# First layer's edge loop: the product of keys and queries is kept in PSUM, and the next gathers wait for the product

## The chip, the cores and the metric

The kernel runs on one core of a Trainium2 chip. Its time is the device time in microseconds (us) of the whole program. TensorE (PE) multiplies matrices from SBUF into PSUM, VectorE (DVE) and ScalarE (ACT) work element by element on SBUF and PSUM, GpSimd (POOL) here mostly issues indirect DMAs (gathers by a list of row numbers), and SyncE (SP) issues plain DMAs. Each engine runs its own instructions in their written order and waits on semaphores that other engines raise.

## The reference, cut to what matters

The model has four pairs of a graph layer and an expert layer on 6250 nodes with 256 features. The first graph layer is an attention over 100,000 edges with 4 heads of 64 features. For an edge from node s to node d and a head h it takes a score q[d,h]·k[s,h] / 8, makes a softmax of the scores over all the edges that end in d, and sums the values v[s,h] with these weights into node d. So each edge needs the 256 keys and the 256 values of its source node, and the 256 queries of its target node. Everything else of the model (seven more layers) is as before and is not touched by the change.

## The kernel before, in words

The edges are sorted by target block beforehand. A tile is 128 edges, one per partition; a *quad* is `Q = 4` tiles. `edge_attend` handles `n = 208` quads. For quad q the engines do this:

- **POOL, `gather` (L2817 to L2827).** Four indirect DMAs, one for each tile, bring 512 floats per edge: first the 256 values, then the 256 keys. They land in `ring`, which has two lanes (even and odd quads, `LANE_SETS = 2`) of seven slots, 260 floats apart. A row is 512 floats long, so the keys of quad q lie where the values of quad q+2 are to go. Hence `gather` of quad q first waits until the keys of quad q-2 are no longer needed: L2819 waits for `val_ready` to count the scores of quad q-2. L2821 waits until the slot's old values have been summed.
- **DVE, `onehot` (L2988)** makes the one-hot matrices `s4` of edges against the nodes of their block.
- **PE, `turn_s` (L2891)** turns them, **ACT, `copy_st` (L2836)** copies them to SBUF, and **PE, `query` (L2900)** multiplies them with the queries: `qe` holds for every edge the queries of its target. `qe` is in PSUM and has two halves, for even and odd quads; a half is 128 x 1024 floats. L2898 waits before it overwrites the half of quad q-2.
- **DVE, `score`.** L2993 waits for the gathered rows, L2998 multiplies the keys with `qe` and puts the product over the keys in `ring` (semaphore `prod_own`), and L3001 sums 64 products for each head and edge into `val` (semaphore `val_ready`).
- Every fourth quad (`closes`), **DVE** finds the running maximum along the sorted list by scans (`within`, `across`, `under`), with small matmuls of **PE** and two exponentials of **ACT** in between. The result is a weight for each edge and head, and a factor `fade` for what has been summed so far.
- **ACT, `widen` (L2867) and `weigh` (L2876, 16 instructions, and L2877)** multiply the values in `ring` by the weights.
- **PE, `collect` (L2948)** sums the weighted values by target: for each tile of the quad one matmul into `o`, which has two banks (`BK = 2`). It waits for the addition of the tile two before (L2947).
- **DVE, `add` (L3081)** adds each of these four results to the accumulator `l_acc`; L3070 and L3072 apply `fade` on every fourth quad.

**What sets the order.** There is no planner. Each engine's program is written out by `steps` (L72): step s issues, for each stage with its lag, the work of quad s - lag. Stages that are plain functions are issued where the list is made, ahead of those that are generators; generators take turns, one piece each up to their next `yield`. So step s is, on PE: `turn_s`(s-1), the small matmuls, two `collect` matmuls of quad s-11, two `query` matmuls of quad s-2, one `collect`, two `query`, one `collect`. On DVE step s is: `onehot`(s), the product of quad s-4, the first addition (or `fade`) of quad s-12, a piece of a scan, then the reduce of quad s-4 (L3001), and the other additions and scan pieces in turn. On POOL it is `gather`(s). `lead = n + 16` means that all 208 quads are written out, with no loop on the chip. A barrier stands at the end of the phase, so the next stage begins when the last engine is done.

Of the kernel before, what the change touches and what calls it, by code (L numbers as in the profile page):

```python
# [11 lines left out]
ALU = mybir.AluOpType  # L12
ACT = mybir.ActivationFunctionType
AX = mybir.AxisListType
# [57 lines left out]
def steps(eng, n, stages, lead=4, tail=0, unroll=2, in_order=False):  # L72

    total = n + max(lag for lag, _ in stages)
    if not in_order:  # L80
        stages = sorted(stages, key=lambda s: -s[0])

    def emit(s, slot, peeled):
        turns = [fn(s - lag, (slot - lag) % unroll) for lag, fn in stages if not peeled or 0 <= s - lag < n]
        turns = [t for t in turns if t is not None]
        while turns:
            turns = [t for t in turns if next(t, turns) is not turns]

    rounds = max(0, (n - lead - tail) // unroll)
    for s in range(min(lead, total)):  # L90
        emit(s, s % unroll, True)
    if rounds:
        with eng.Fori(0, rounds) as i:
            for k in range(unroll):
                emit(i * unroll + (lead + k), (lead + k) % unroll, False)
    for s in range(lead + unroll * rounds, total):
        emit(s, s % unroll, True)
# [2003 lines left out]
def blocks_of(nc, engine, L, q, tiles=Q):  # L2101

    _, vals = nc.values_load_multi_w_load_instructions(L.block[0:1, ds(q * tiles, tiles)], engines=(engine,),
                                                       min_val=0, max_val=T - 1,
                                                       skip_runtime_bounds_check_because="made below T on chip")
    return vals
# [649 lines left out]
LANE_SETS = 2  # L2756
# [3 lines left out]
def edge_attend(nc, core, L, name, table, queries, acc, scale):  # L2760

    H, W, n, CQ, U, BK = 4, D, L.quads, 4, 14, 2
# [5 lines left out]
    with Phase(nc, name) as ph:  # L2768
        ring = ph.sb("ring", [P, LANE_SETS * Q, LANE])

        def rows(q, a, b):
            at, lane = q // LANE_SETS % LANE_SLOTS * LANE_STEP, q % LANE_SETS * Q
            return ring[:, lane:lane + Q, at + a:at + b]
# [21 lines left out]
        qe = ph.ps("qe", [P, 2, Q, W])  # L2795
# [18 lines left out]
        with nc.Block() as block:  # L2814
            @block.gpsimd
            def _(pool):
                def gather(q, slot):  # L2817
                    if q >= LANE_SETS:
                        pool.wait_ge(val_ready, q - LANE_SETS + 1)  # L2819
                    if q >= AWAY:  # L2820
                        pool.wait_ge(out_done, (q - AWAY + 1) * Q)  # L2821
                    pool.sem_inc(taken, 1)
                    for j in range(Q):
                        t = q * Q + j
                        pool.indirect_dma_start(rows(q, 0, 2 * D)[:, j, :], None, table,  # L2825
                                                bass.IndirectOffsetOnAxis(ap=L.src[:, t:t + 1], axis=0)
                                                ).then_inc(got[q % LANE_SETS], 16)  # L2827
                steps(pool, n, [(0, gather)], **whole)
# [51 lines left out]
            @block.tensor  # L2880
            def _(pe):
                for k in range(2):
                    pe.matmul(o[0:1, k, 0:half], core.ident[:, P - 1:P], L.dst[:, k * half:(k + 1) * half],
                              start=True, stop=True).then_inc(lasts, 1)

                def turn_s(q, slot):
                    pe.wait_ge(s_ready, q + 1)
                    if q:
                        pe.wait_ge(st_ready, q)
                    for j in range(Q):  # L2890
                        ins = pe.transpose(stp[:, j, :], s4[:, slot, j, :], core.ident_b[:])  # L2891
                    ins.then_inc(st_turned, 1)

                def query(q, slot):
                    b = blocks_of(nc, mybir.EngineType.PE, L, q)
                    pe.wait_ge(st_ready, q + 1)
                    if q >= 2:
                        pe.wait_ge(prod_own, q - 1)  # L2898
                    for j in range(Q):
                        ins = pe.matmul(qe[:, q % 2, j, :], st[:, j, :],  # L2900
                                        queries[:, ds(b[j], 1), :].rearrange("p o d -> p (o d)"), start=True, stop=True)
                        if j == 1:
                            yield
                    ins.then_inc(q_done, 1)

                def flip(q, slot):
                    if closes(q):
                        c = q // CQ
                        pe.wait_ge(val_ready, q + 1)
                        if c:  # L2910
                            pe.wait_ge(scanned, c * PER)
                            pe.wait_ge(weight_ready, c)
                        pe.transpose(score_t, val[:, c % 2].rearrange("p h t -> p (h t)"), core.ident[:])
                        pe.wait_ge(copied, c + 1)
                        pe.transpose(dst_t, dst4[:].rearrange("p h t -> p (h t)"), core.ident[:]).then_inc(flipped, 1)

                def meet(q, slot):
                    if closes(q):
                        c = q // CQ
                        pe.wait_ge(scanned, c * PER + 3)  # L2920
                        if c:
                            pe.wait_ge(fade_ready, c)
                        pe.matmul(ends_p[:, :, :, 0], behind[:, 0:1], core.ident[0:RW, 0:RW], start=True, stop=True)
                        pe.matmul(ends_p[:, :, :, 1], ahead[:, P - 1:P], core.ident[0:RW, 0:RW], start=True, stop=True
                                  ).then_inc(met, 1)

                def reach_back(q, slot):
                    if closes(q):
                        c = q // CQ
                        pe.wait_ge(scanned, c * PER + 11)  # L2930
                        for k in range(2):
                            pe.matmul(reach_p[:, k:k + 1], az[:, k, :], core.ones[0:1, 0:1], start=True, stop=True)
                        pe.matmul(fade_p, first[:], drop, start=True, stop=True).then_inc(reached, 1)

                def lower(q, slot):
                    if closes(q):
                        c = q // CQ
                        pe.wait_ge(scanned, (c + 1) * PER)
                        pe.transpose(wp, far[:], core.ident[0:RW, 0:RW]).then_inc(lowered, 1)

                def collect(q, slot):
                    pe.wait_ge(wide_ready, q + 1)
                    pe.wait_ge(weighed, q + 1)
                    for j in range(Q):
                        t = q * Q + j
                        if t >= BK:
                            pe.wait_ge(acc_own, t - BK + 1)  # L2947
                        pe.matmul(o[:, t % BK, 0:W + H], sf[:, q % 2, j, :], rows(q, 0, W + H)[:, j, :], start=True, stop=True  # L2948
                                  ).then_inc(out_done, 1)
                        if j:  # L2950
                            yield
                steps(pe, n, [(11, collect), (1, turn_s), (2, query), (4, flip), (5, meet), (6, reach_back), (7, lower)], **whole)

            @block.vector
            def _(dve):
# [35 lines left out]
                def score(q, slot):  # L2991
                    c, t0 = q // CQ, q % CQ * Q
                    dve.wait_ge(got[q % LANE_SETS], 16 * Q * (q // LANE_SETS + 1))  # L2993
                    dve.wait_ge(q_done, q + 1)
                    if c >= 2 and q % CQ == 0:
                        dve.wait_ge(flipped, c - 1)
                    k = rows(q, W, 2 * W)
                    dve.tensor_tensor(k, k, qe[:, q % 2], ALU.mult).then_inc(prod_own, 1)  # L2998
                    yield
                    dve.wait_ge(prod_own, q + 1)  # L3000
                    dve.tensor_reduce(val[:, c % 2, :, t0:t0 + Q].rearrange("p h q -> p q h"),  # L3001
                                      k.rearrange("p q (h c) -> p q h c", h=H), AX.X, ALU.add).then_inc(val_ready, 1)

                def within(q, slot):
                    if not closes(q):
# [56 lines left out]
                def add(q, slot):  # L3062
# [12 lines left out]
                    for j in range(Q):  # L3075
# [5 lines left out]
                        dve.tensor_tensor(a, a, o[:, t % BK, 0:W + H].unsqueeze(1), ALU.add).then_inc(acc_own, 1)  # L3081
                        yield
                steps(dve, n, [(4, score), (12, add), (0, onehot), (5, within), (6, across), (7, under)], **whole)


# [1622 lines left out]
```

## Time and profile before

| | |
|---|---|
| median of 3 runs | 8400.12 us (8380.09 to 8412.67) |
| the profiled execution: its own time | 8395.49 us |
| its span | 8393.8 us |
| busy share of the span | PE 70%, PEld 53%, DVE 63%, ACT 37%, POOL 62% |
| `edge_attend`, first gather to last product | about 650 to 1948 us of the span |

The span is the time from the first to the last instruction. Busy shares are means over the whole program; the stage of the change is some 15% of it. "PEld" is the load of weights by PE, which overlaps its matmuls. In the rows of the profile "idle before" is the time that an engine stood still just before an instruction, and the arrow names what ended that wait; "issue" is time in which it waited for nothing that the profile shows. The tile names in the rows leave out numbers, so `l0_edges_ring` appears as `l_edges_ring`.

### The profile page before, as it was taken

The numbers are of one execution on the slowest core, as the hardware profiler recorded it, in microseconds if no ns is written. First come the engines' busy times: TensorE is split into PE (matmuls) and PEld (weight loads), VectorE is DVE, ScalarE is ACT, GpSimd is POOL, SyncE is SP. The second block draws the span as 40 slices with busy tenths as digits, with TensorE's granted clock in tenths as the row PEclk, the third lists the DMA queues.
The fourth block names the chain that finished last, engine by engine and source line by source line (L and its number), as shares of the span: only waits on it lengthen the run. The fifth ranks groups of instructions, "written<-read, shape, count | busy, mean of one in ns | idle before, by whom it ended". The sixth has DMA issues, their size and how long they took to land. (4 is left out here: it accounts for less than half of the span.)

```text
span 8393.8 us, 114926 instructions
## 1 busy us (share of the span) xinstructions
PE 5911.5 (70%) x29083; PEld 4485.9 (53%) x29083; DVE 5252.3 (63%) x14320; ACT 3102.5 (37%) x9138; POOL 5186.5 (62%) x5153
## 2 busy tenths in 40 slices
PE   6586777774399555556688888965577775574398
PEld 5234555553387234444577777754455553453387
DVE  9867888887665576665544444446677777435544
ACT  1245888887422300000333333312344444312322
POOL 0475666665577677777677777756777771433422
PEclk9798999996599877778699999967789986686599
DMA  5475666563366333333111111116333343473366
GB/s 147 152 247 160 171 173 172 170 172 115 108 207 200 111 102 101 100 102 103 28 28 32 31 28 32 26 27 193 102 105 103 105 100 117 150 229 95 100 204 199
DMA packets 633946, 1017.21 MB, mean 121 GB/s; under 512 B 136434, under 2 KB 436482, under 8 KB 631948
## 3 DMA queue, kind: packets, MB, share of 16 engines
q0 software_dynamic: 241920, 540.19, 24.2%
q1 hardware_dynamic: 391436, 470.18, 17.7%
q8 instruction: 245, 4.01, 0.2%
q14 instruction: 345, 2.83, 0.1%
HBM read 790.98 MB, written 222.86 MB: 121 GB/s over the span
## 5 line engine op out<-in xcount | busy, mean ns | idle before, releaser
L4099 POOL DMA_INDIRECT gat_edges_rows<-gat_table,gat_room x1080 | 1115.5, 1033 | 340.9 <-issue 322.4
L2825 POOL DMA_INDIRECT l_edges_ring<-pairs,first_room x832 | 843.8, 1014 | 472.5 <-issue 242.2
L2387 POOL DMA_INDIRECT l_sum_rows<-l_feats,back_room x832 | 827.0, 994 | 265.7 <-issue 241.9
L2407 PE MATMUL l_sum_o<-l_sum_rows,l_sum_s 128*128 128x256 f32 x1664 | 604.4, 523 | 468.3 <-DVE l_sum_s L2418 220.4
L2876 ACT ACTIVATE l_edges_ring<-l_edges_ring,l_edges_weight 128x64 f32<-128x64 f32 x3328 | 816.4, 335 | 0.0
L2407 PEld LDWEIGHTS l_sum_o<-l_sum_rows,l_sum_s 128*128 128x128 f32 x1664 | 410.9, 261 | 655.0 <-DVE l_sum_s L2418 325.5
L2948 PE MATMUL l_edges_o<-l_edges_ring,l_edges_sf 128*128 128x260 f32 x1664 | 534.9, 427 | 149.8 <-DVE l_acc L3081 141.1
L3717 ACT ACTIVATE m_ffn_ht<-m_ffn_hp,m_ffn_b1t 128x256 f32<-128x256 f32 (+1 forms) x598 | 270.7, 453 | 815.5 <-PE m_ffn_hp L3684 810.3
L2429 DVE TENSOR_TENSOR l_acc<-l_acc,l_sum_o 128x256 f32 x832 | 350.1, 421 | 351.3 <-PE l_sum_o L2407 258.4
L3694 PE MATMUL m_ffn_yp<-m_ffn_w2b,m_ffn_ht 128*128 128x256 f32 x2156 | 502.1, 385 | 30.4 <-ACT m_ffn_ht L3717 29.8
L3684 PE MATMUL m_ffn_hp<-m_ffn_xt,m_ffn_w1b 128*128 128x256 f32 (+1 forms) x2392 | 509.0, 366 | 11.5 <-DVE m_ffn_xt L3733 7.2
L2503 POOL DMA_INDIRECT x_all<-l_feats,main_room x432 | 424.2, 982 | 131.6 <-issue 124.0
L258 POOL DMA_INDIRECT main_records<-l_proj_carried x400 | 404.1, 1010 | 153.5 <-issue 121.3
L2503 POOL DMA_INDIRECT l_edges_rows<-l_feats,main_room x400 | 391.5, 979 | 122.1 <-issue 116.0
L3684 PEld LDWEIGHTS m_ffn_hp<-m_ffn_xt,m_ffn_w1b 128*128 128x128 f32 x2392 | 422.8, 193 | 80.5 <-ACT m_ffn_ht L3717 16.8
L2900 PE MATMUL l_edges_qe<-x_all,l_edges_st 128*128 x1664 | 456.3, 400 | 2.1 <-DVE l_edges_ring L2998 1.1
L3694 PEld LDWEIGHTS m_ffn_yp<-m_ffn_w2b,m_ffn_ht 128*128 128x128 f32 x2156 | 399.7, 190 | 103.3 <-ACT m_ffn_ht L3717 34.9
L3949 PE MATMUL gat_edges_hp<-l_acc,gat_edges_w1b 128*128 128x256 f32 (+1 forms) x1600 | 421.8, 411 | 36.2 <-DVE gat_edges_a_parts L4271 23.3
L2948 PEld LDWEIGHTS l_edges_o<-l_edges_ring,l_edges_sf 128*128 128x128 f32 x1664 | 293.7, 199 | 274.3 <-DVE l_acc L3081 223.1
L3962 PE MATMUL gat_edges_yp<-gat_edges_w2b,gat_edges_ht 128*128 128x256 f32 x1568 | 422.5, 417 | 0.0
L3081 DVE TENSOR_TENSOR l_acc<-l_acc,l_edges_o 128x260 f32 x832 | 340.8, 410 | 126.3 <-PE l_edges_o L2948 111.2
L1987 PE MATMUL l_proj_op<-l_proj_w,l_proj_zt 128*128 128x512 f32 (+1 forms) x784 | 371.0, 600 | 34.7 <-DVE l_proj_osb L2069 34.4
(899 smaller groups left out, 14604.4 us busy)
## 6 DMA issues: line engine op xcount, KB each, us to landing
sorted_rows<-l_proj_zero SPq DMA_DIRECT2D x44, 1032.0 KB
m_ffn_w1b<-in_L_ffn_w SPq DMA_DIRECT2D x32, 1024.0 KB, 6.4
m_ffn_w2b<-in_L_ffn_w SPq DMA_DIRECT2D x32, 1024.0 KB, 5.4
m_ffn_xs<-sorted_rows SPq DMA_DIRECT2D x120, 258.0 KB, 3.6
m_ffn_w1b<-in_L_ffn_W SPq DMA_DIRECT2D x57, 512.0 KB, 4.6
m_ffn_w2b<-in_L_ffn_W SPq DMA_DIRECT2D x57, 512.0 KB
m_by_node<-gat_edges_ys SPq DMA_DIRECT2D x96, 256.0 KB
l_proj_taken<-m_by_node SPq DMA_DIRECT2D x28, 768.0 KB, 6.9
```

Source lines behind the costliest of these rows:

```text
L2387: pool.indirect_dma_start(rows[:, slot, j, :], None, table, bass.IndirectOffsetOnAxis(ap=L.src[:, t:t + 1], axis=0)).then_inc(got[slot], 16)
L2407: pe.matmul(o[:, j, 0:D], s4[:, q % S4, j, :], rows[:, slot, j, :], start=True, stop=True).then_inc(out_done, 1)
L2503: pool.indirect_dma_start(rows(q)[:, j, :], None, table, bass.IndirectOffsetOnAxis(ap=L.src[:, t:t + 1], axis=0)).then_inc(got[q % GS], 16)
L2825: pool.indirect_dma_start(rows(q, 0, 2 * D)[:, j, :], None, table, bass.IndirectOffsetOnAxis(ap=L.src[:, t:t + 1], axis=0)).then_inc(got[q ...
L2876: act.activation(v, v, ACT.Identity, scale=p[:, h, t0 + j:t0 + j + 1])
L2900: ins = pe.matmul(qe[:, q % 2, j, :], st[:, j, :], queries[:, ds(b[j], 1), :].rearrange("p o d -> p (o d)"), start=True, stop=True)
L2948: pe.matmul(o[:, t % BK, 0:W + H], sf[:, q % 2, j, :], rows(q, 0, W + H)[:, j, :], start=True, stop=True).then_inc(out_done, 1)
L3684: ins = pe.matmul(hp[:, k % HB, 0:n], w1b[:, par, c, k * P:(k + 1) * P], xt[:, par, c, 0:n], start=(c == 0), stop=(c == DC - 1))
L3694: ins = pe.matmul(yp[:, par, h, :], ht[:, par, k, h * P:(h + 1) * P], w2b[:, par, k, :], start=(k == 0), stop=(k == HC - 1))
L3949: ins = pe.matmul(self.hp[:, j, 0:n * P], self.w1b[:, c, k * P:(k + 1) * P], self.zt[:, t:t + n, c * P:(c + 1) * P], start=(c == 0), stop= ...
L3962: ins = pe.matmul(self.yp[:, h, :], self.ht[:, q % 2, k, h * P:(h + 1) * P], self.w2b[:, k, :], start=(k == 0), stop=(k == self.HC - 1))
L4099: pool.indirect_dma_start(rows[:, slot, j, :], None, table, bass.IndirectOffsetOnAxis(ap=L.src[:, q * B + j:q * B + j + 1], axis=0)).then_ ...
```

## The change

The product of keys and queries is written over the queries in `qe` (PSUM) and no longer over the keys in `ring` (SBUF), and the reduce reads it there. The keys in `ring` are then read for the last time by the product, so POOL's gather of quad q waits for the product of quad q-2 and no longer for its scores. In return `qe`'s half is in use until the reduce has read it, so PE's `query` of quad q waits for the scores of quad q-2 and no longer for its product.

```diff
@@ -2816,7 +2816,7 @@
                 def gather(q, slot):
                     if q >= LANE_SETS:
-                        pool.wait_ge(val_ready, q - LANE_SETS + 1)
+                        pool.wait_ge(prod_own, q - LANE_SETS + 1)
@@ -2895,7 +2895,7 @@
                     pe.wait_ge(st_ready, q + 1)
                     if q >= 2:
-                        pe.wait_ge(prod_own, q - 1)
+                        pe.wait_ge(val_ready, q - 1)
@@ -2994,12 +2994,12 @@
-                    k = rows(q, W, 2 * W)
-                    dve.tensor_tensor(k, k, qe[:, q % 2], ALU.mult).then_inc(prod_own, 1)
+                    prod = qe[:, q % 2]
+                    dve.tensor_tensor(prod, rows(q, W, 2 * W), prod, ALU.mult).then_inc(prod_own, 1)
                     yield
                     dve.wait_ge(prod_own, q + 1)
                     dve.tensor_reduce(val[:, c % 2, :, t0:t0 + Q].rearrange("p h q -> p q h"),
-                                      k.rearrange("p q (h c) -> p q h c", h=H), AX.X, ALU.add).then_inc(val_ready, 1)
+                                      prod.rearrange("p q (h c) -> p q h c", h=H), AX.X, ALU.add).then_inc(val_ready, 1)
```

## Rows read from the trace of the kernel before

**Rows 1.** Busy time of each engine in a stretch of the edge loop.
```profile
700.00:1900.00 1200.00, 945.27 (x4512) 683.70 (x4512) 1026.76 (x2231) 1000.92 (x3853) 794.81 (x784) 0.95 0.61 172
```
**Rows 2.** Waits from 700 to 1900 us: total us, times, longest us.
```profile
PE l_edges_o L2948 <- DVE l_acc L3081: 131.6, 112, 4.9
ACT l_edges_st L2836 <- PE l_edges_qe L2900: 111.1, 90, 6.5
DVE l_acc L3081 <- PE l_edges_o L2948: 91.5, 142, 2.1
...
DVE l_edges_ring L2998 <- DMA l_edges_ring<-pairs,first_room: 68.8, 68, 3.2
ACT l_edges_weight L2861 <- PE l_edges_turned L2939: 42.0, 49, 1.3
ACT l_edges_far L2851 <- PE l_edges_turned L2915: 40.5, 49, 2.8
```
**Rows 3.** POOL's gathers from 700 to 1900 us, grouped by line.
```profile
L2825 POOL DMA_INDIRECT l_edges_ring<-pairs,first_room x784 | 796.0, 1015 | 405.5 <-issue 229.7 <-DVE l_edges_val L3001 173.5 <-PE l_edges_o L2948 2.4
```
**Rows 4.** The product's line, whole run: durations in ns, its waits, its waiters.
```profile
L2998 DVE TENSOR_TENSOR l_edges_ring<-l_edges_ring,l_edges_qe x208: 1200/1215/1223, 681.8 to 1947.0; 128x1024 f32<-128x1024 f32 x104
...
  DMA l_edges_ring<-pairs,first_room: 78.9, 74
...
  PE l_edges_qe L2900: 1.1, 2
```
**Rows 5.** The reduce's line, whole run, and who waited for it.
```profile
L3001 DVE TENSOR_REDUCE l_edges_val<-l_edges_ring x208: 1192/1202/1221, 683.0 to 1948.5; 128x16 f32<-128x1024 f32 x104
...
  POOL l_edges_ring L2825: 204.3, 121
```
**Rows 6.** Timeline, DVE: start us, us, then the instruction and its idle time.
```profile
1293.49 1.22 DVE L2998 TENSOR_TENSOR l_edges_ring<-l_edges_ring,l_edges_qe 128x1024 f32<-128x1024 f32 x1
...
1295.37 1.20 DVE L3001 TENSOR_REDUCE l_edges_val<-l_edges_ring 128x16 f32<-128x1024 f32 x1
...
1305.33 1.22 DVE L2998 TENSOR_TENSOR l_edges_ring<-l_edges_ring,l_edges_qe 128x1024 f32<-128x1024 f32 x1 [0.83 <-DMA l_edges_ring<-pairs,first_room]
...
1310.62 1.22 DVE L2998 TENSOR_TENSOR l_edges_ring<-l_edges_ring,l_edges_qe 128x1024 f32<-128x1024 f32 x1 [0.35 <-DMA l_edges_ring<-pairs,first_room]
```
**Rows 7.** Timeline, POOL, of the same stretch.
```profile
1294.70 0.95 POOL L2825 DMA_INDIRECT l_edges_ring<-pairs,first_room  x1 [0.30 <-issue]
1297.37 0.94 POOL L2825 DMA_INDIRECT l_edges_ring<-pairs,first_room  x1 [1.73 <-DVE l_edges_val L3001]
...
1301.60 0.94 POOL L2825 DMA_INDIRECT l_edges_ring<-pairs,first_room  x1 [0.30 <-issue]
1302.85 0.95 POOL L2825 DMA_INDIRECT l_edges_ring<-pairs,first_room  x1 [0.30 <-issue]
```
**Rows 8.** Timeline: a long stop of POOL, and the product behind it.
```profile
1354.89 0.94 POOL L2825 DMA_INDIRECT l_edges_ring<-pairs,first_room  x1 [3.37 <-issue]
...
1361.19 1.22 DVE L2998 TENSOR_TENSOR l_edges_ring<-l_edges_ring,l_edges_qe 128x1024 f32<-128x1024 f32 x1 [3.08 <-DMA l_edges_ring<-pairs,first_room]
```
**Rows 9.** Timeline: the first quads of the loop.
```profile
692.66 1.22 DVE L2998 TENSOR_TENSOR l_edges_ring<-l_edges_ring,l_edges_qe 128x1024 f32<-128x1024 f32 x1 [4.31 <-DMA l_edges_ring<-pairs,first_room]
...
694.13 2.98 PE L2900 MATMUL l_edges_qe<-x_all,l_edges_st 128*128 x8 [0.89 <-DVE l_edges_ring L2998]
...
697.34 1.22 DVE L2998 TENSOR_TENSOR l_edges_ring<-l_edges_ring,l_edges_qe 128x1024 f32<-128x1024 f32 x1 [1.60 <-DMA l_edges_ring<-pairs,first_room]
```
**Rows 10.** DVE groups, whole run: count, busy us, mean ns, idle before.
```profile
L3081 DVE TENSOR_TENSOR l_acc<-l_acc,l_edges_o 128x260 f32 x832 | 340.8, 410 | 126.3 <-PE l_edges_o L2948 111.2 <-DVE l_acc L3081 11.8 <-issue 2.4
...
L4283 DVE TENSOR_TENSOR gat_edges_sf<-row,gat_room 128x1024 f32<-128x1024 f32 x135 | 163.9, 1214 | 1.0
...
L2663 DVE TENSOR_REDUCE l_edges_top<-l_edges_mx 128x4 f32<-128x512 f32 x208 | 142.8, 687 | 18.5 <-issue 18.3
...
L3070 DVE TENSOR_TENSOR l_acc<-l_acc,l_edges_minor 128x256 f32 x52 | 21.8, 419 | 0.4 <-DVE l_acc L3081 0.4
```

## The prediction

> **What bounds the kernel now.** The change touches one stage, so I read that stage alone: first the windows view, then the waits and the groups, then the timeline for the mechanism. From 700 to 1900 us 196 quads pass (784 gathers of four, [rows 3]), 1200 / 196 = 6.12 us each. No engine is full: DVE is busy 1026.8 of 1200 us, ACT 1000.9, PE 945.3, and POOL's gathers take 794.8 and the fixed stop of about 0.3 us between two of them another 229.7 [rows 1, 3]. So the pace is set by engines that wait for each other, and the question is which wait ends last. DVE is the fullest. The reader should see that its idle 173 us are nearly all two waits: 68.8 us in front of the product, for gathered rows that have not landed, and 91.5 us in front of the additions, for PE's summing matmuls [rows 2]. Over the whole loop the first of them is 78.9 us in 74 places [rows 4]. POOL for its part stands 173.5 us (204.3 in the whole loop, 121 times) until DVE's reduce releases it [rows 3, 5]. This makes a circle: DVE's reduce, POOL's four gathers, landing, product, reduce.
>
> The timeline shows the circle closing late. The reduce of 1295.37 ends at 1296.57, and 0.80 us later, at 1297.37, POOL begins the next gather, after 1.73 us of standing. Its fourth DMA ends at 1302.54, and the product that needs it can start at 1305.33, 2.79 us later, having waited 0.83 us. POOL takes the gather after it with no wait, at 1302.85, and that too lands late: the product of 1310.62 waits 0.35 us [rows 6, 7].
>
> **The change part by part.** (1) *POOL is released by the product.* In the same rows the product ends at 1294.71. Plus 0.80 us is 1295.51, and POOL is itself free at 1294.70 + 0.95 + 0.30 = 1295.95. So the gather starts at 1295.95, 1.42 us earlier, and lands at about 1303.9, before 1305.33 - 0.83 = 1304.50, when DVE was ready for it. The next gather also starts 1.42 us earlier, more than the 0.35 us that were missing. In this pattern both waits go. What is late next on this circle: 0.80 + 5.23 of gathers + 2.79 + 1.22 of product = 10.0 us for two quads, well under 12.2, and POOL by itself needs (796.0 + 229.7) / 196 = 5.23 us a quad [rows 3]. So POOL does not become the bound.
>
> Not all of the 78.9 us can go. POOL makes a stop of about 3.4 us now and then, which no semaphore explains; behind the one shown the product waits 3.08 us [rows 8]. There are seven such stops in the loop, one in 28 quads. With gathers up to 1.8 us earlier (1296.57 - 1294.71 = 1.86 us from the product's end to the reduce's in [rows 6]) each leaves about 1.2 us, together 8.4. The very first wait, 4.31 us for quad 2 [rows 9], loses one reduce and keeps about 3. That leaves 12, so 78.9 - 12 = 67 us are freed on DVE.
>
> (2) *DVE's two instructions work on PSUM.* The product already reads PSUM; new are its writing there and the reduce's reading. For the reading there are rows. From SBUF 1024 elements take 1214 ns and 256 take 419, so an element takes 795 / 768 = 1.035 ns [rows 10]. A reduce of 1024 from SBUF takes 1202 ns, so one of 512 would take 1202 - 530 = 672; the one from PSUM takes 687, 15 ns more [rows 5, 10]. A product with one operand in PSUM takes 1215 ns and one of the same size from SBUF alone 1214; an addition of 260 with PSUM takes 410 ns and one of 256 without 419 [rows 4, 10]. So reading PSUM costs between -9 and +15 ns. For writing PSUM by DVE the trace has no row. Its low end is the same -9 ns; its high end is a second pass over the 1024 elements, since now both reading and writing meet in one bank: about 1.07 us (1024 times 1.035 ns). I take 15 ns for it, by the reduce's rows as the nearest, and 15 for the reduce: 208 x 0.030 = 6 us, all on DVE and so on the path.
>
> Here a rule of the Trainium skill speaks against the change. "VectorE: DVE Perf Modes", section on the TRN2 errata, gives VectorE a fixed cost of 58 cycles from SBUF and 120 from PSUM; at its 0.96 GHz an estimate by that page is 65 ns more for the reduce, 13 us in the loop where the rows give 3. The trace does not agree with it: 15 ns on the reduce, none on the product.
>
> (3) *PE's queries wait for the reduce.* Behind that wait stand two more queries, a summing matmul and PE's whole next step, and for them DVE's additions and ACT's copies. But by the order of step s the queries of quad s-2 need the reduce of quad s-4, which DVE issues in its step s, and they stand behind a `collect` that needs the last addition of quad s-12, which DVE issues later in that same step. What PE waits for anyway comes after the reduce, so the new wait cannot end last. Only before quad 11 is nothing collected. There the query of 694.13 waited for the product of 692.66 [rows 9] and would now wait for a reduce 1.3 us later, but the product it feeds comes later than 697.34 + 1.22, and its queries would be done by 694.13 + 1.3 + 2.98 = 698.4. Cost: nothing; if that cover were gone, 1.25 us for each of some eight quads, 10 us.
>
> (4) *The ring's other wait* (old values summed) ended last twice, for 2.4 us in all [rows 3]. Gathers come 1.9 us earlier against a wait that is fulfilled a step before: nothing.
>
> (5) *What the others give back.* If DVE did only without its DMA waits, 1200 - 68.8 = 1131 us would be left for these 196 quads. ACT without its waits for the queries needs 1200 - 111.1 = 1089: its 42.0 and 40.5 us for the small matmuls are a fixed delay within each fourth step. PE without its waits for the additions needs 1200 - 131.6 = 1068 [rows 2]. So the next limit lies only 42 us behind the first, and single quads with scans will meet it before the mean does. In the places where PE waits for DVE an earlier DVE passes on at once; where DVE waits for PE (142 places) it partly will not. I take off 11 us of the 67, about one in six, by judgement.
>
> Sum: -67 + 6 + 11 = -50 us, from 8395.5 of the profiled execution to 8345. The median of the runs shown is 4.6 us above it, so I forecast 8350 us.
>
> **The rivals.** (A) *All of it arrives*: PSUM is free and ACT and PE follow. Then 67 to 79 us go, 8321 to 8333. For it: POOL stood for 204 us, so its reserve is large, and PE and ACT each have over 100 us of waits on others. Against it: ACT's reserve of 42 us.
> (B) *A wait moves and little changes*: DVE's DMA waits come back as waits in front of the additions, because ACT, with 1089 of the 1131 us, falls behind in the quads that have scans. Then 0 to 35 us go, 8365 to 8400. For it: DVE already waits more for PE than for DMA. Against it: where ACT waits for the queries it waits 1.2 us a time (111.1 / 90), so it is usually early.
> (C) *Slower*: the product in place in PSUM streams slowly, reading and writing one bank. Up to 0.35 us a quad (68.8 / 196) it is paid by the DMA waits removed; above that, at L2998 alone, the kernel is slower. At the full second pass DVE needs 1131 / 196 + 1.07 = 6.84 us a quad against 6.12, 0.72 x 208 = 150 us more: 8550. For it: no row shows such a write. Against it: reading and writing `l_acc` at one address in SBUF costs nothing to be seen (410 ns for 260) [rows 10].
> (D) *The change doesn't do what it says*: POOL would be held by something else, such as landings that get slower as gathers crowd. The DMA engines are busy 0.61 of this stretch at 172 GB/s [rows 1], and at the new pace it is 180, so I give it no price beyond (B)'s.
>
> **How the numbers follow.** My forecast with its neighbourhood (8338 to 8362) has 0.45, (A) 0.22, (B) with (D) 0.27, (C) 0.06. The range from 8315 to 8405 holds (A), the forecast, (B) and the runs' own scatter, and leaves out (C) and some scatter at either end. A change of this kernel's time can be told from none beyond about 0.5%, 42 us, that is below 8358 or above 8442. Below 8358 lie (A) and some 0.37 of my forecast's 0.45 and a little of the rest: faster 0.60. Same is 0.34, slower 0.06.
>
> **What would show it.** In the changed kernel's profile: POOL's waits for DVE fall from 173.5 to under 60 us; the product's waits for DMA fall from 68.8 to under 15, those that remain being behind POOL's long stops; the product and the reduce stay within 1200 to 1260 ns; PE's queries never wait for `val_ready` after the first quads; the last product comes at about 1895 and not 1947 us, and everything after it is only shifted. I am wrong if the additions' wait for PE grows from 91.5 by more than 30 us (B), or if the product is longer than 1.5 us (C).

## The result, and the profile after

| | before | changed |
|---|---|---|
| median | 8393.03 us (7 runs) | 8307.97 us (7 runs, 8298.73 to 8350.08) |
| ratio to before | | 0.9905, 95% interval 0.9886 to 0.9924 |
| the same kernel timed again on another chip | 8419.4 us (11 runs) | 8329.28 us (6 runs), ratio 0.9882 (0.9862 to 0.9902) |
| span of the profiled execution | 8393.8 us | 8300.1 us |
| edge loop, first to last product | 1265.2 us | 1186.0 us |
| DVE's waits for DMA in front of the product, whole run | 78.9 us | 24.7 us |
| DVE's waits for PE in front of the additions, whole run | 111.2 us | 90.9 us |

The kernel became faster by 85 us. I forecast 50, with a range that began at 8315, so the direction was right and the time fell 7 us outside. Of the 93.7 us between the two spans 79 are in the edge loop; the other 15 lie in stages that are not touched, and are no more than the scatter of single runs: behind the last addition the runs of this document take between 6390 and 6450 us, whichever kernel they run.

The windows view of the changed kernel, to be held against [rows 1]: time, then busy us of PE, PEld, DVE, ACT and POOL, granted clock, DMA share, GB/s.

```profile
700.00:1800.00 1100.00, 884.13 (x4418) 650.82 (x4417) 1001.16 (x2185) 973.15 (x3772) 766.09 (x766) 0.98 0.65 184
```

DVE is now busy for 91% of the stretch (86% before), ACT 88% (83%). The granted clock rose from 0.95 to 0.98: at two levels, 1.2 and 2.4 GHz, that is 10% of the time at the lower one before and 4% after. The waits of the same stretch, which answer to [rows 2]:

```profile
PE l_edges_stp L2891 <- ACT l_edges_st L2836: 139.7, 178, 2.3
...
POOL l_edges_ring L2825 <- PE l_edges_o L2948: 103.5, 135, 1.1
...
DVE l_acc L3081 <- PE l_edges_o L2948: 68.6, 137, 1.8
ACT l_edges_st L2836 <- PE l_edges_qe L2900: 49.8, 58, 6.0
PE l_edges_o L2948 <- DVE l_acc L3081: 48.3, 55, 3.1
...
POOL l_edges_ring L2825 <- DVE l_edges_qe L2998: 27.6, 25, 3.0
DVE l_edges_qe L2998 <- DMA l_edges_ring<-pairs,first_room: 18.2, 13, 2.4
```

The two stretches hold nearly the same number of quads (196 and 191.5). PE's stands for DVE's additions shrank from 131.6 us in 1200 to 48.3 in 1100, and those for ACT's copy grew from 85.4 to 139.7: DVE no longer comes last everywhere. POOL's wait fell from 173.5 + 2.4 to 103.5 + 27.6. The first of these two is put down to PE, and would be the wait for the ring's old values. The timeline speaks against that. In it, POOL's starts and DVE's products (the second row is DVE's):

```profile
1306.62 0.94 POOL L2825 DMA_INDIRECT l_edges_ring<-pairs,first_room  x1 [0.95 <-PE l_edges_o L2948]
...
1304.59 1.22 DVE L2998 TENSOR_TENSOR l_edges_qe<-l_edges_ring,l_edges_qe 128x1024 f32<-128x1024 f32 x1
```

The product ends at 1305.81 and POOL starts 0.81 us later, the same distance as before the change (0.80 us). Over the whole loop POOL stands longer than its fixed 0.3 us in front of 89 gathers that the view puts down to PE, and 88 of these start 0.81 us behind the end of the product of the quad two before (90.6 of 91.6 us). So nearly all of it is the product; a PE matmul merely ended near it. The groups of the two instructions that moved, over the whole run:

```profile
L2998 DVE TENSOR_TENSOR l_edges_qe<-l_edges_ring,l_edges_qe 128x1024 f32<-128x1024 f32 x208 | 253.2, 1217 | 28.5 <-DMA l_edges_ring<-pairs,first_room 24.7 <-PE l_edges_qe L2900 3.7
...
L3001 DVE TENSOR_REDUCE l_edges_val<-l_edges_qe 128x16 f32<-128x1024 f32 x208 | 250.9, 1206 | 0.2
```

Writing the product to PSUM, over one of its inputs, costs 3 ns on average (1214 to 1217) and reducing from there 3 ns (1203 to 1206).

**Slow matmuls.** At the lower clock the same matmuls take nearly twice as long. PE's timeline before; a query row is four instructions:

```profile
1313.96 0.71 PE L2948 MATMUL l_edges_o<-l_edges_ring,l_edges_sf 128*128 128x260 f32 x2 [2.06 <-DVE l_acc L3081]
...
1319.26 1.03 PE L2900 MATMUL l_edges_qe<-x_all,l_edges_st 128*128 x4
...
1322.25 0.39 PE L2932 MATMUL l_edges_turned<-ones,l_edges_cuts 1*64 1x1 f32 x4 [0.58 <-DVE l_edges_first L3039]
...
1324.66 1.91 PE L2900 MATMUL l_edges_qe<-x_all,l_edges_st 128*128 x4
```

I call a quad slow if such a row, or one of the summing matmuls, is at least 1.45 times its usual length in it. The kernel before has 28 slow quads of 208, the changed one 9. The granted clock says the same: within the loop it lies at the lower level in 30 stretches, 119.5 us together, and in the changed kernel in 11, 44.4 us. In the kernel before PE stands for DVE's addition once in four quads, for 2.05 us on average, and in the changed one for 1.05. The slow row above comes 11 us behind such a stand, and right behind a short one. Of the 26 places from 760 us on at which slow rows begin, 12 come right behind a stand of 1.9 to 4.9 us, and 13 of the other 14 have a stand of about 2 us one or two quads before.

### The profile page after: what moved, and what is told of

The parts are those of the page before. It is cut to its first block and busy times, and to the rows that moved or that the text cites. A ratio compares the mean times of both kernels' runs of the same rounds, so it can differ in the third digit from the quotient of the medians.

```text
span 8300.1 us, 114926 instructions
## 1 busy us (share of the span) xinstructions
PE 5867.7 (71%) x29083; PEld 4459.0 (54%) x29083; DVE 5251.0 (63%) x14320; ACT 3095.0 (37%) x9138; POOL 5170.4 (62%) x5153
## 3 DMA queue, kind: packets, MB, share of 16 engines
q0 software_dynamic: 241920, 540.19, 24.7%
## 5 line engine op out<-in xcount | busy, mean ns | idle before, releaser
L2948 PE MATMUL l_edges_o<-l_edges_ring,l_edges_sf 128*128 128x260 f32 x1664 | 516.8, 415 | 62.2 <-DVE l_acc L3081 54.8
L2503 POOL DMA_INDIRECT x_all<-l_feats,main_room x432 | 422.1, 977 | 131.6 <-issue 124.3
L3684 PEld LDWEIGHTS m_ffn_hp<-m_ffn_xt,m_ffn_w1b 128*128 128x128 f32 x2392 | 421.4, 193 | 80.9 <-ACT m_ffn_ht L3717 17.1
L3081 DVE TENSOR_TENSOR l_acc<-l_acc,l_edges_o 128x260 f32 x832 | 339.6, 408 | 106.1 <-PE l_edges_o L2948 90.9
L2747 DVE TENSOR_TENSOR l_acc<-l_acc,l_edges_o 128x257 f32 x832 | 348.6, 419 | 72.7 <-PE l_edges_o L2607 52.0
```

Source lines behind the costliest of these rows:

```text
L2503: pool.indirect_dma_start(rows(q)[:, j, :], None, table, bass.IndirectOffsetOnAxis(ap=L.src[:, t:t + 1], axis=0)).then_inc(got[q % GS], 16)
L3684: ins = pe.matmul(hp[:, k % HB, 0:n], w1b[:, par, c, k * P:(k + 1) * P], xt[:, par, c, 0:n], start=(c == 0), stop=(c == DC - 1))
```

## The experiments

"Loop" is the time from the first to the last product, and like slow quads it is read from one profiled execution; the changed kernel, taken twice, has 1186.0 and 1182.7 us with 9 and 5 slow quads. DMA waits are DVE's in front of the product, PE waits those in front of the product and of the additions, both over the whole run.

| kernel | ratio to before (95%) | loop us | DMA waits | PE waits | slow quads |
|---|---|---|---|---|---|
| before | 1 | 1265.2 | 78.9 | 115 | 28 |
| changed | 0.9905 (0.9886 to 0.9924) | 1186.0 | 24.7 | 95 | 9 |
| e1 product in PSUM only | 1.0019 (1.0005 to 1.0032) | 1271.6 | 82.0 | 120 | 31 |
| e3 before, reduce at once | 1.0045 (1.0028 to 1.0061) | 1298.4 | 19.0 | 173 | 8 |
| e7 changed, late for q % 4 = 3 | 0.9979 (0.9967 to 0.9991) | 1257.8 | 68.0 | 118 | 29 |
| e8 changed, early for q % 4 = 3 only | 0.9975 (0.9961 to 0.9990) | 1260.1 | 73.1 | 118 | 32 |
| e13 before, reduce later | 0.9994 (0.9977 to 1.0012) | 1265.1 | 130.5 | 47 | 13 |
| e12 changed, reduce later | 0.9940 (0.9917 to 0.9963) | 1222.8 | 23.4 | 110 | 33 |
| e11 changed, additions first | 1.0040 (1.0026 to 1.0054) | 1309.2 | 13.6 | 227 | 86 |
| e6 before, PE's stand filled | 0.9999 (0.9981 to 1.0018) | 1254.6 | 83.9 | 103 | 16 |
| e17 the same, filled twice | 0.9977 (0.9961 to 0.9992) | 1262.7 | 86.2 | 105 | 15 |
| e10 changed, filled | 0.9889 (0.9863 to 0.9915) | 1183.0 | 23.3 | 96 | 6 |
| e9 changed, 12 one-hot slots | 0.9894 (0.9871 to 0.9918) | 1178.3 | 23.8 | 89 | 5 |
| e4 e9 with two st | 0.9900 (0.9878 to 0.9923) | 1182.9 | 25.5 | 95 | 5 |
| e16 e12 and e4 together | 0.9953 (0.9932 to 0.9973) | 1226.7 | 24.9 | 112 | 37 |
| e18 e16, filled | 0.9886 (0.9865 to 0.9906) | 1188.8 | 25.8 | 77 | 4 |
| e19 e16, filled by half | 0.9890 (0.9869 to 0.9911) | 1175.9 | 24.5 | 70 | 2 |

How quads are cut matters little for the slow ones: cut at PE's own steps their numbers in the loop move by up to six, except in e11, where the 86 become 47. By the granted clock, the loop of e11 has 49 stretches at the lower level, and those of e16, e18 and e19 have 38, 6 and 4 (146.8, 23.9 and 17.1 us).

**PSUM without the release (e1).**

```diff
-                        pool.wait_ge(prod_own, q - LANE_SETS + 1)
+                        pool.wait_ge(val_ready, q - LANE_SETS + 1)
```

> The changed kernel with one line put back: POOL's gather again waits for the scores (val_ready). So the product is written to and reduced from PSUM, and nothing is released earlier. Theory 1 (the whole gain is POOL's earlier release): the gathers' timing is that of the kernel before, the product and reduce cost 9 ns more a quad (1221 + 1205 against 1215 + 1202 ns), 2 us in 208 quads; ratio to before 0.999 to 1.002, DMA waits in front of the product about 79 us. Rival (leaving the ring's SBUF alone is itself worth something, as the gain of 85 us is more than the 54 us by which those DMA waits fell): ratio 0.994 to 0.998.

Measured 1.0019, slower by 0.05 to 0.32%: PSUM alone brings nothing and the whole gain hangs on POOL's release. The rival is out. The slow quads stayed too (31).

**Only some gathers released early (e7, e8).** In e7 the line reads as shown; e8 has the two semaphores exchanged.

```diff
-                        pool.wait_ge(prod_own, q - LANE_SETS + 1)
+                        pool.wait_ge(val_ready if q % 4 == 3 else prod_own, q - LANE_SETS + 1)
```

> The changed kernel, but the gathers of quads with q % 4 == 3 wait for the scores again. Theory 1 with the pattern of the trace (POOL stood 2.1 us before such a gather and both this one and the next landed late): most of the gain is lost, ratio to before 0.996 to 0.999, DMA waits 50 to 75 us. Rival (each quad's earlier release is worth the same): a quarter is lost, ratio 0.992 to 0.994.

> The changed kernel, but only the gathers of quads with q % 4 == 3 are released by the product; the other three in four wait for the scores, as before. It is the counterpart of the run in which only those were held back, which kept 0.2 of the 0.95% gain. Theory 1 with the pattern (one gather in four matters): ratio to before 0.991 to 0.994. Rival (the gathers share one budget, and any that is late costs): 0.995 to 0.998.

e7 came as theory 1 had it: holding back one gather in four loses four fifths. But e8, releasing that one alone, gains 0.25% and not 0.7%; its rival was right. The two parts give 0.21 and 0.25% apart and 0.95% together. In e8's trace the wait has moved to the gather behind it, which then waits for its own scores: DVE's waits for DMA in front of quads with q % 4 = 0 are 1.2 us on average, those in front of q % 4 = 3 are gone. So of these two gathers in a row, one on each lane, both must be early: in e7 only the first of them was late, in e8 the first was early and the second late. That these two alone would be enough was not run. And both e7 and e8 kept the slow matmuls (29 and 32 quads), which went only when both waits did.

**The place of the reduce and of the additions (e3, e13, e12, e11).** e3 takes the yield between product and reduce out (and puts one behind the reduce), e13 and e12 put a second one in, in the kernel before and in the changed one; e11 lists the additions first (its list is cut at the dots).

```diff
@@ e13 and e12 @@
                     yield
+                    yield
                     dve.wait_ge(prod_own, q + 1)
@@ e11 @@
-                steps(dve, n, [(4, score), (12, add), (0, onehot), ...
+                steps(dve, n, [(12, add), (4, score), (0, onehot), ...
```

> The kernel before with the yield between product and reduce moved behind the reduce: the scores are ready about 0.55 us earlier (1.68 us after the product's end on average before, about 1.13 now), with no PSUM and no new wait, and the first addition comes 1.1 us later. Theory 1: a third of the earlier release, so DMA waits fall from 79 to about 50 us and the ratio is 0.996 to 0.998. Rival (PE's wait for the first addition sets the pace as much as the gathers): PE's waits for additions grow and the ratio is 1.000 to 1.006.

> The kernel before with the same yield: the reduce comes behind the second addition, and there POOL waits for it, some 0.8 us longer. Theory 1 and 3 together: what the earlier addition gives is less than what the later release takes; DMA waits in front of the product grow from 79 to over 130 us and the ratio is 1.002 to 1.010. Rival (the order of the additions matters more than the release, as the run with the reduce at once suggests): ratio 0.993 to 0.999.

e3 is the most telling of these. The waits for DMA fell to 19.0 us, lower than in the changed kernel, and still it is 0.45% slower. Its waits from 700 to 1800 us:

```profile
PE l_edges_o L2948 <- DVE l_acc L3081: 195.8, 170, 3.7
...
DVE l_acc L3081 <- PE l_edges_o L2948: 130.7, 212, 2.1
...
DVE l_edges_ring L2998 <- DMA l_edges_ring<-pairs,first_room: 14.3, 12, 2.5
```

The first addition now comes behind the reduce; PE stands for it, then DVE for PE. The rival was right. Slow matmuls are not the reason: e3 has only 8 slow quads, though from 760 us on PE stands 47 times for more than 1.45 us. e13 does the opposite: DMA waits up by 52 us as expected, waits for PE down from 115 to 47, slow quads down from 28 to 13, and in sum nothing (0.9994, between the ranges of theory and rival). So there are two circles, one over POOL and one over PE, and in the kernel before each of the three places of the reduce that were run is a trade between them. The change takes the reduce out of the first circle without moving it in the second.

> The changed kernel with one more yield between product and reduce: the reduce comes behind the second addition and not ahead of it. POOL's release is the product's and stays. Theory 3: the second addition is ready 1.1 us earlier, PE goes on sooner, and the reduce covers PE's matmuls for the third and fourth; DVE's waits for PE fall below 70 us and the ratio to before is 0.985 to 0.990. Rival (DVE stands at the second addition instead, or the scans that need the scores become late): ratio 0.990 to 0.995.

> The changed kernel with the additions ahead of the score stage in each of DVE's steps: the first addition (or fade) comes before the product and not behind it. Theory 3 (after the change the pace is set by the circle of DVE's first addition, PE's third summing matmul and queries, ACT's copy): PE's waits for additions fall, the product comes some 0.4 us later, for which POOL has reserve, and the time falls by 5 to 30 us against the changed kernel, ratio to before 0.987 to 0.990. Rival (PE has not finished the first summing matmul when DVE comes to it, so DVE now stands where it did the product): DVE's waits for PE grow from 91 us by 50 or more and the ratio is 0.995 or above.

Both are worse than the changed kernel, and both have more slow quads, 33 and 86. In e11 the rival was right: DVE stands for PE 227 us. In e12 the rival had the time (0.9940), but neither side had the cause. Taken over its quads that are not slow alone, its period is 5.67 us, less than the changed kernel's 5.71 counted in the same way; its 31 slow quads in the middle of the loop take 1.4 to 1.8 us more than others of the same place.

**The clock (e6, e17, e10, e18, e19).** These repeat query matmuls, with the same operands into the same place, where PE stands anyway; only PE's work grows, by 2 or 4 of 16 query matmuls.

```diff
@@ e6 and e10; e17 with (0, 1, 0, 1) @@
                         if j == 1:
+                            if q % 4 == 1:
+                                for i in range(2):
+                                    pe.matmul(qe[:, q % 2, i, :], st[:, i, :], queries[:, ds(b[i], 1), :] ...)
                             yield
@@ e18; e19 with range(2) @@
+                    if q % 4 == 1:
+                        yield
+                        for i in range(Q):
+                            ins = pe.matmul(qe[:, q % 2, i, :], st[:, q % 2, i, :], queries[:, ds(b[i], 1), :] ...)
                     ins.then_inc(q_done, 1)
```

> The kernel before, with two of the four query matmuls of every fourth quad (q % 4 == 1) done twice, in the place where PE otherwise stands for DVE's first addition (2.05 us each time). The repeated matmuls write the same values again. Theory 2 (PE's long stands are followed by matmuls at the granted 1.2 GHz, in 28 quads before and 9 after the change, and this is the part of the gain that the DMA waits do not explain): quads with slow matmuls fall from 28 to under 12 and the time falls by 10 to 25 us, ratio 0.997 to 0.999, though PE does some 50 us more work. Rival (the slow matmuls are only a sign, or come regardless): their number stays above 20 and the ratio is 1.000 to 1.004.

> The kernel before, with two of the four query matmuls of every fourth quad (q % 4 == 1) done three times, 2.06 us of repeated work, in the place where PE otherwise stands for DVE's first addition, 2.05 us on average. With half of this fill the quads with slow matmuls went from 28 to 16 and the loop from 1265 to 1255 us. Theory 2 (the clock is worth about 1 us for each such quad): they fall below 12, the loop to 1245 to 1255 us, ratio 0.997 to 0.999. Rival (the fill is late where PE's stand was short, and takes back what the clock gives): ratio 1.000 to 1.004.

e6 is inconclusive (0.9999, interval from 0.9981), and its slow quads fell to 16, not below 12. e17 is faster than the kernel before, beyond its interval, with some 100 us more work for PE, and its ratio is in theory 2's range; but its slow quads (15) and its loop (1262.7, 2.5 us shorter than before) are not. So in the kernel before itself the clock's part is seen only faintly.

> The kernel with two buffers for st and the reduce behind the second addition (0.9953, 37 quads with slow matmuls, loop 1226.7 us), with the four query matmuls of every fourth quad (q % 4 == 1) done a second time behind the last summing matmul of that step, ahead of PE's longest stand. By its quads without slow matmuls alone that loop would take 1164 us. Theory 2 (its 37 slow quads are the whole reason why it is slower than the changed kernel): they fall below 15 and the loop below 1195 us, ratio 0.987 to 0.991. Rival (they fall and the loop stays above 1215, or they do not fall because the engine's other stands suffice): ratio 0.994 to 0.998.

> The last kernel (two buffers for st, the reduce behind the second addition, repeated query matmuls behind the last summing matmul of every fourth step) with two repeated matmuls and not four, 1.03 us of PE and not 2.06. With four, 4 quads had slow matmuls, the loop took 1188.8 us, and DVE stood 35 us for the repeated matmuls themselves, since the queries count as done only behind them. Theory 2: half the fill is enough for the clock and DVE's 35 us mostly go: under 12 slow quads, loop 1165 to 1182 us, ratio 0.984 to 0.988. Rival (half the fill leaves a stand long enough): above 20 slow quads, loop above 1200 us, ratio 0.990 or more.

For e16 this settles it. The windows of e16 and of e18, in this order:

```profile
700.00:1800.00 1100.00, 874.42 (x4262) 670.18 (x4262) 975.84 (x2111) 936.93 (x3648) 751.46 (x743) 0.94 0.62 178
```

```profile
700.00:1800.00 1100.00, 930.87 (x4795) 725.96 (x4795) 1005.30 (x2183) 965.97 (x3766) 764.53 (x765) 0.99 0.65 184
```

Nothing but repeated matmuls was added. The granted clock goes from 0.94 to 0.99, slow quads from 37 to 4, the loop from 1226.7 to 1188.8 us, and the ratio from 0.9953 to 0.9886, although DVE now stands 35 us for the repeated matmuls themselves. With half the fill (e19) 2 slow quads are left and the loop takes 1175.9: 50.8 us less for 35 slow quads, 1.45 us each. Slow quads and loop are as theory 2 had them; the ratio, 0.9890, is not (0.984 to 0.988). What PE did before its slow matmuls in e16:

```profile
1316.27 0.38 PE L2891 MATMUL l_edges_stp<-ident_b,l_edges_s 128*128 128x128 bf16 x4 [1.52 <-ACT l_edges_st L2836]
...
1319.92 0.71 PE L2948 MATMUL l_edges_o<-l_edges_ring,l_edges_sf 128*128 128x260 f32 x2
1322.39 0.39 PE L2891 MATMUL l_edges_stp<-ident_b,l_edges_s 128*128 128x128 bf16 x4 [1.76 <-ACT l_edges_st L2836]
...
1323.02 1.75 PE L2948 MATMUL l_edges_o<-l_edges_ring,l_edges_sf 128*128 128x260 f32 x4
1324.56 1.91 PE L2900 MATMUL l_edges_qe<-x_all,l_edges_st 128*128 x4
```

A stand of 1.76 us, and then 1.75 and 1.91 us for what takes 1.15 and 1.03. "TensorE: Matmul & The Clock Gate" of the Trainium skill, in the section on oscillation in real kernels, describes stands of PE that drop its clock again and again, so that the work behind them is slow too. The trace agrees in that, with shorter stands: that page's are waits of 3 to 5 us for DMA.

The stand of 1.52 us one quad earlier is part of it. In e16, from 760 us on, PE stands about 1.5 us for ACT's copy in 48 places, once in four quads, and about 1.76 us in 40, each one quad behind; 31 of the 36 beginnings of slow rows come right behind the second. In e18 and e19 the repeated matmuls fill the second, and the 48 first ones stay. In e19:

```profile
1298.09 1.03 PE L2907 MATMUL l_edges_qe<-x_all,l_edges_st 128*128 x4
1300.02 0.38 PE L2891 MATMUL l_edges_stp<-ident_b,l_edges_s 128*128 128x128 bf16 x4 [0.90 <-ACT l_edges_st L2836]
...
1316.61 0.38 PE L2891 MATMUL l_edges_stp<-ident_b,l_edges_s 128*128 128x128 bf16 x4 [1.52 <-ACT l_edges_st L2836]
```

So a stand of 1.52 us once in four quads is not enough, and the length of a single stand doesn't foretell the lower clock.

> The changed kernel with two of the four query matmuls of every fourth quad (q % 4 == 1) done twice, where PE otherwise stands for DVE's first addition (1.03 us each time in the changed kernel, 2.05 in the kernel before). Theory 2 (the clock): little is left to win, quads with slow matmuls go from 9 to 3 to 9, and the extra 50 us of PE work costs nothing or a little; ratio to before 0.989 to 0.994. Rival (PE's time is on the path after the change, as its stands have shrunk): ratio above 0.994.

Nearly as expected (0.9889, the range began at 0.989): with 9 slow quads there is little to win, and the ratio stays within the changed kernel's own scatter.

**Room on PE and ACT (e4, e9, e16).** e4 has all of the edit below, e9 only its last hunk, and e16 is e4 with e12's second yield.

```diff
-        st = ph.sb("st", [P, Q, P])
+        st = ph.sb("st", [P, 2, Q, P])
-                    if q:
-                        act.wait_ge(q_done, q)
-                    act.copy(st[:], stp[:]).then_inc(st_ready, 1)
+                    if q >= 2:
+                        act.wait_ge(q_done, q - 1)
+                    act.copy(st[:, q % 2], stp[:]).then_inc(st_ready, 1)
...
-                        ins = pe.matmul(qe[:, q % 2, j, :], st[:, j, :],
+                        ins = pe.matmul(qe[:, q % 2, j, :], st[:, q % 2, j, :],
...
-    H, W, n, CQ, U, BK = 4, D, L.quads, 4, 14, 2
+    H, W, n, CQ, U, BK = 4, D, L.quads, 4, 12, 2
```

> The changed kernel with two buffers for the turned one-hot matrices (st), so that ACT's copy needs the queries of quad q-2 and not of q-1; to make room the one-hot ring has 12 slots and not 14. In the changed kernel PE stands 139.7 us in 1100 for ACT's copy, and ACT 49.8 us for PE's queries. Theory 3 (the pace is now that of the circle query, copy, turn, query): both waits fall, to under 60 and under 10 us, quads with matmuls at 1.2 GHz stay below 12, ratio to before 0.984 to 0.989. Rival (DVE, busy 91% of the stretch, is the bound now, so these waits cost nothing): ratio 0.989 to 0.992.

> The changed kernel with 12 slots of the one-hot ring and not 14, nothing else: the control of the runs that have this beside another edit. Both theories: no difference from the changed kernel, ratio to before 0.989 to 0.992.

> The changed kernel with two buffers for st (12 one-hot slots) and the reduce behind the second addition. With the later reduce alone the profile had 33 quads with matmuls at 1.2 GHz, behind stands of PE of 1.75 us for ACT's copy, and 0.994. Theory 2 and 3: two buffers take these stands away, quads with slow matmuls fall below 12 and with them the loss; ratio 0.982 to 0.988, the best of all. Rival (the later reduce is itself worse, whatever the clock): ratio 0.991 to 0.995.

ACT's wait for the queries went entirely, and the time stayed: 0.9900 against 0.9894 of the control. ACT's waits for the queries do not bound the changed kernel. PE still stood 119.2 us for ACT's copy where e4's theory had under 60, so of these stands e4 says little. That DVE with its 91% is the bound is likely, but no run made DVE's work smaller. e16's theory was wrong too: two buffers did not take PE's stands away, since PE stood for DVE's one-hot matrices and ACT's full queue as well.

> The changed kernel itself, timed beside the run above on one chip. All theories: ratio to before 0.989 to 0.992, loop 1180 to 1190 us, 5 to 10 quads with slow matmuls.

Loop and slow quads came as expected; the ratio, 0.9882, lies just below its range, which its interval overlaps. e10, e18, e19 and the changed kernel can't be told apart (0.9882 to 0.9905), so no version here is shown to beat the changed one.

## Why the prediction was right or wrong

1. *POOL released by the product.* Right, and e1 shows it is all there is. In size: 54 us of waits for DMA went, not 67. Seven waits of the loop's first ten quads, 11.7 us, stayed, where I had kept 3 us: there POOL issues without a wait on anyone, so its own pace is the bound. The seven long stops of POOL left 9.8 us together, as estimated (8.4).
2. *PSUM.* 6 ns a quad where I took 30: 1 us and not 6. Rival C is out, and so is the estimate of 65 ns more for the reduce, by "VectorE: DVE Perf Modes" of the Trainium skill: measured were 3 ns.
3. *PE's queries.* Right: PE stood 1.0 us, once, for the reduce.
4. *The ring's other wait.* Right: the view names PE 103.5 us, but by the distance to the products nearly all of that is a wrong name. It means that one sign of the prediction did not come: POOL's waits for DVE should have fallen below 60 us, and with the right name they are near 118 (27.6 and some 90). They cost nothing: by the prediction's own figures POOL needs 5.23 us a quad and the loop now takes 5.7, so POOL must stand somewhere.
5. ***"What the others give back": this step failed, in its sign.*** I took off 11 us because DVE's waits for PE would grow. They fell by 20 us, 31 us away from my forecast. I had counted the engines' reserves as if their speeds were fixed. Part of the miss seems plain, though only e1 bears on it: with the release alone put back, PE's waits return to 120 us and the slow quads to 31, so both hang on POOL's late release. The way from there is argued and not shown: PE's stands for DVE's additions get shorter when DVE is earlier, and with them the delays of the queries and of the copy behind them. The other part is the clock: PE worked at 1.2 GHz in 28 quads, and then DVE stood for slow matmuls. How much this is of the 79 us can only be estimated: 19 fewer slow quads at 1.45 us (e16 to e19) are 28 us; slow quads against others of the same place in the two traces give 12 us. What it gives shows in DVE's waits for PE, of which 19 us went in the loop, so 28 is probably too much. e18 and e19 show that slow quads cost time, in e16; for the kernel before there is only e17's 0.23%. The size stays open.

The account of DVE between its first and its last product closes: 54.2 us fewer of DMA waits, 19.1 of waits for PE at the additions, 0.9 of other and shorter stands, and 5.0 of busy time, 1078.1 to 1073.1, make the 79. The fall in busy time is not cheaper work, as the durations of DVE's instructions add up to the same (1233.8 and 1233.7 us); more of them overlap where no wait is between them. Against the 50 us of my sum: part 1 was 13 too high, the 6 for PSUM are already in the busy time, part 5 was off by 30, and 6 for overlap and short stands were no term at all; 50 - 13 + 6 + 30 + 6 = 79. My sum without the 11 taken off and with 5 less for PSUM would have been 66 us and 8334; the clock, 12 to 28 us by the estimates above, was missing from every rival. The range was too narrow at the low end for that reason: its end assumed that nothing could be better than all waits for DMA gone. Of the other signs, the waits for DMA came down to 18.2 us in 1100 and not below 15, the last product came at 1869 us and not at 1895, and the two instructions, the queries and the additions' waits came as forecast.

## What to carry to other kernels

Release a buffer at its last reader, even if that reader then has to put its result elsewhere: the release, not the place, was worth 1%. When two engines' waits feed each other, a wait removed takes more than itself along; look at which of PE's stands hang on it, and whether matmuls behind those stands run at the lower clock, before you bound the gain by the wait alone. And test a release per buffer set: here three gathers in four gave 0.2%, the fourth alone 0.25%, and all of them 1%.

## What the runs showed of the hardware that I had not expected

- Repeating matmuls in PE's stands made kernels faster: 0.9953 to 0.9886 with some 100 us more PE work, by the granted clock (0.94 to 0.99).
- VectorE writes 128x1024 f32 to PSUM in place over one of its inputs in 1217 ns, as it does to SBUF (1214).
- Two stands of 1.52 and 1.76 us in successive quads, once in about 24 us, went with the 1.2 GHz level behind most of them (e16, 38 stretches); with the second filled and the first left, 4 to 6 such stretches remained (e18, e19).
